# Weight rounding of a feed-forward layer moved within an attention stage, one VectorE operation per slot

## What is computed

```python
x = _layernorm(x + _L0_attn_ref(x, ...))   # 16 heads, causal, power-law decay
x = _layernorm(x + _L0_ffn_ref(x, w_gate, w_up, w_down))
x = _layernorm(x + _L1_attn_ref(x, ...))   # gated delta rule
x = _layernorm(x + _L1_ffn_ref(x, ...))

scores = jnp.einsum('bhnd,bhmd->bhnm', Q, K) / jnp.sqrt(jnp.float32(dk))
scores = scores + power_law_mask(N, DECAY_SCALE)[None, None]
attn = jax.nn.softmax(scores, axis=-1)

def fp4_quant_dequant(x):                  # blocks of 16 along the last dimension
    scale = jnp.max(jnp.abs(xb), axis=-1, keepdims=True) / 6.0
    scale = jnp.maximum(scale, jnp.float32(1e-12))
    xn = xb / scale
    idx = jnp.searchsorted(_MID, jnp.abs(xn))
    q = _GRID[idx] * jnp.sign(xn) * scale
```

## Time and profile before

| | |
|---|---|
| median of three runs | 3314.37 us (3314.29 to 3314.68) |
| profiled execution | 3316.07 us, span in the profile 3314.3 us |
| TensorE busy | 3003.8 us, 91% of the span |
| VectorE busy | 2307.2 us, 70% |
| ScalarE busy | 1222.2 us, 37% |
| GpSimd busy | 1022.4 us, 31% |
| mean granted TensorE clock | 0.96 of full |
| attention stage | about 0 to 658 us of the span |

### The profile page before, as it was taken

How to read it: one execution, slowest core, us unless ns; L and a number is a source line. 1 busy time by engine, 2 the same in 40 slices (tenths; PEclk the granted TensorE clock), 3 DMA queues, 4 the chain that set the end, 5 groups by cost and what they waited for, 6 DMA issues and landing times. The chain is left out here.

```text
span 3314.3 us, 81973 instructions
## 1 busy us (share of the span) xinstructions
PE 3003.8 (91%) x33019; PEld 2075.3 (63%) x33019; DVE 2307.2 (70%) x5231; ACT 1222.2 (37%) x2943; POOL 1022.4 (31%) x1495
## 2 busy tenths in 40 slices
PE   6999999599987999989999989999999999998897
PEld 3444444256655677677667767767776776776565
DVE  4666677778865776776776776777677677676466
ACT  2343333233333433343343343344344334332354
POOL 2454555348852221222221221221222122121011
PEclk8999999699988999999999999999999999998899
DMA  2111111000011110010010010000001001000000
GB/s 80 40 51 33 33 29 33 14 1 1 1 28 29 43 34 18 18 31 21 17 31 18 21 31 18 21 23 26 21 18 30 18 21 30 18 18 2 2 26 26
DMA packets 94040, 80.43 MB, mean 24 GB/s; under 512 B 54992, under 2 KB 68320, under 8 KB 93664
## 3 DMA queue, kind: packets, MB, share of 16 engines
q1 hardware_dynamic: 93664, 75.18, 8.4%
HBM read 57.70 MB, written 4.85 MB: 19 GB/s over the span
## 5 line engine op out<-in xcount | busy, mean ns | idle before, releaser
L1814 PE MATMUL gd_bk<-gd_xT,gd_wh 128*128 128x512 f32 x768 | 398.1, 628 | 22.1 <-DVE gd_L L1582 14.2
L480 DVE TENSOR_REDUCE at_nm<-at_ring 128x2 f32<-128x256 f32 (+3 forms) x256 | 199.2, 820 | 144.6 <-PE at_ring L623 144.6
L1528 DVE SCALAR_TENSOR_TENSOR gd_YK<-gd_bk,gd_cw,gd_YK 128x511 f32<-128x511 f32 (+2 forms) x384 | 282.8, 742 | 11.8 <-ACT gd_YK L1401 6.2
L1586 DVE COPY_PREDICATED gd_U<-gd_mU,gd_bk 128x256 f32<-128x256 int32 x320 | 140.9, 442 | 209.3 <-PE gd_bk L2016 149.5
L1994 PE MATMUL gd_bk<-gd_L,gd_NT 64*64 64x64 f32 x5120 | 212.5, 225 | 64.0 <-DVE gd_L L1588 41.3
L2011 PE MATMUL gd_bk<-gd_U,gd_ZS 64*64 64x64 f32 x5120 | 211.3, 225 | 39.4 <-ACT gd_ZS L1494 39.3
L1483 ACT COPY gd_O<-gd_bk 64x128 f32<-64x128 f32 x448 | 108.6, 260 | 356.9 <-PE gd_bk L1952 355.9
L1994 PEld LDWEIGHTS gd_bk<-gd_L,gd_NT 64*64 64x64 f32 x5120 | 177.9, 137 | 97.4 <-DVE gd_L L1588 55.8
L1494 ACT COPY gd_ZS<-gd_bk 128x256 f32<-128x256 f32 x320 | 115.2, 370 | 328.2 <-PE gd_bk L1994 324.9
L2011 PEld LDWEIGHTS gd_bk<-gd_U,gd_ZS 64*64 64x64 f32 x5120 | 178.4, 138 | 85.4 <-ACT gd_ZS L1494 43.5
L302 POOL TENSOR_TENSOR at_PT<-at_PT,at_dm 128x1024 f32<-128x1024 f32 (+3 forms) x128 | 198.0, 1547 | 10.7
(11 more groups left out here) (353 smaller groups left out, 6922.2 us busy)
## 6 DMA issues: line engine op xcount, KB each, us to landing
gd_wh<-in_L_attn_W_qkvz SPq DMA_DIRECT2D x64, 512.0 KB, 3.6
gd_gb<-gates SPq DMA_DIRECT2D x128, 64.0 KB, 3.3
X<-in_L_attn_x SPq DMA_DIRECT2D x8, 512.0 KB, 8.7
at_QT<-at_QS SPq DMA_DIRECT2D x128, 32.0 KB, 2.0
at_KT<-at_KS SPq DMA_DIRECT2D x128, 32.0 KB, 2.0
at_OC<-at_Ob SPq DMA_DIRECT2D x128, 32.0 KB, 2.0
at_RC<-inverse SPq DMA_DIRECT2D x128, 32.0 KB, 1.8
out_x<-X SPq DMA_DIRECT2D x8, 512.0 KB, 2.9
```

Of the source, the lines that this page charges most:

```text
L480: nc.vector.tensor_reduce(nm[v % 2][:, k, c0:c0 + HS + 1:HS], set_of(s, 2 + p)[:, :, 0:n], AX.X, ALU.max).then_inc(max_done, 1)
L1528: nc.vector.scalar_tensor_tensor(out[:, s:W], bank_[:, 0:W - s], cw[:, j, head(f, e), CONVK - 1 - s:CONVK - s], out[:, s:W], ALU.mult, ALU ...
L1586: last = nc.vector.copy_predicated(U[e][:, :, :], wide(mU[l]), chunks(A_[e], 1))
L1814: ins = nc.tensor.matmul(out[:, :], wh[e][:, k, col * DK:(col + 1) * DK], xT[:, k, :], start=k == 0, stop=k == DC - 1)
```

## The change

Three things, all in the attention:

- The steps start at unit 4 and not at unit 18, one in each slot, so that all 110 are done at unit 31, slot 1. Units 32 and 33 do none.
- Inside a slot the step stands between the decay addition (L452) and all else that VectorE does there; before, it stood after the row maxima, the query update and the y and V additions.
- The three loads of the raw weights are issued at units 0, 1 and 2 and not at 6, 8 and 10.

```diff
-    WUNIT = UNITS - 14
+    WUNIT = UNITS - 28
...
-                    if k == 0 and u in (6, 8, 10):
-                        ffn_load(sp, (u - 6) // 2)
+                    if k == 0 and u in (0, 1, 2):
+                        ffn_load(sp, u)
...
-                EARLY = (UNITS - WUNIT) * TPS
 
                 def weight_span(u, k):
 
-                    if u < WUNIT:
-                        return 0, 0
-                    if u < UNITS:
-                        i = (u - WUNIT) * TPS + k
-                        return i, i + 1
-                    if u == UNITS:
-                        a_ = EARLY + min(k, 3) * 8
-                        return (a_, a_ + 8) if k < 3 else (a_, a_)
-                    if u == UNITS + 1 and k < 3:
-                        a_, n_ = EARLY + 24, WALL - EARLY - 24
-                        return a_ + n_ * k // 3, a_ + n_ * (k + 1) // 3
-                    return 0, 0
+                    i = (u - WUNIT) * TPS + k
+                    return i, i + (0 <= i < WALL)
...
                         nc.vector.tensor_tensor(PT[s % RP][:, 0:2, 0:n], set_of(s, 1)[:, :, 0:n],
                                                 ld[:, 0:n].unsqueeze(1).broadcast_to([P, 2, n]), ALU.add).then_inc(add_done, 1)
+                    for i in range(*weight_span(u, k)):
+                        weight_step(i)
                     if k == 3 and has(u - 1) and u % 2 == 0:
...
-                    for i in range(*weight_span(u, k)):
-                        weight_step(i)
                     if g == 2 and seq(b - 1):
```

## The result

The changed kernel takes 3332.01 us (median of five runs, 3328.85 to 3336.46) against 3314.33 us before: slower by 0.55%, ratio 1.0055 with a 95% interval of 1.0041 to 1.007. The profiled execution took 3333.23 us around a span of 3331.5.

The account below looks back on a forecast made before the run. TensorE was taken to bound the attention, paced by first row maxima, a-scores, value product, max scores, next maxima. Costs of 17.2 and 11.5 less gains of 18.9 gave +9.8 us on 3314.37, so 3324.2; range 3305 to 3336.

Parts of the forecast that it names:

- the likeliest case: Four to seven clock drops with the waits as predicted: 3321 to 3330 us, chance 0.45.
- third rival: Each of eight stalls drops the clock and slow matmuls push slot 1's addition into L302: +20.5, 3335 us, chance 0.15.
- Cost 1: Steps ahead of the maxima wait for GpSimd's running operation in units 4 to 28: 17.2 us, bounds 6 and 21.
- Cost 2: Stalls in eight units make TensorE's clock drop, 2.3 us a drop: 11.5 us, bounds 0 and 18.4.
- forms 0 to 3: Of ten repeating step kinds, a reduce and three small operations on 32 columns; a small one in unit 12 costs nothing.
- five of eight: Of eight units with stalls of 1.3 to 2 us, five were taken to drop the clock: 11.5 us.
- The rival without drops: Waits as predicted but no clock drops: -1.7 us, 3312.7 us, chance 0.25.
- Gain 1: The tail without the 54 steps of units 32 and 33: 9.2 us, from waits of 4.9 and 3.7 plus 0.6.
- Gain 2: Units 18 to 27: what the steps in their old places cost comes back, 7.7 us.
- Gain 3: Units 28 to 31: a short step hides better there than the old one, 2 us by estimate, bounds 0 and 4.
- The first rival: No clock drops, waits as predicted: -1.7 us, 3312.7 us; with up to three drops still within 7 us; chance 0.25.
- hidden steps: The wait goes to GpSimd and costs under 6 us, without drops: 3301.5 us, or 3295.5 with no cost; chance 0.15.

Follow-up runs that it names:

- scalar-operation kernel: The changed kernel with 109 of its 110 steps replaced by a scalar multiply and maximum on 32 columns, weights not rounded: 3326.83 us, ratio 1.0043.
- the kernel with both GpSimd operations short: The changed kernel with GpSimd's product L302 and its residual addition L309 both cut to one column: 3297.02 us, ratio 0.9954.
- the planned one: The changed kernel without steps in three slots, two in slots with long idle time, steps in units 2 to 27, loads one unit earlier: 3295.08 us, ratio 0.9943.

## Why the prediction was right, and where it was off

The time, 3332.0, is in the range and on the side that I forecast, and the mechanism is the one that I gave. The size is not: +17.7 us came where my sum said +9.8, and 3332 lies outside the likeliest case's own 3321 to 3330, near the third rival (3335). Two terms were too small, Cost 1 and the number of clock drops in Cost 2. By its steps:

- **What bounds.** First maxima -> a-scores -> next maxima is the order that sets the pace: shown by unit 8, and by the three slots whose step, moved behind the maxima, costs nothing.
- **The wait for GpSimd.** Shown from both sides. Other VectorE operations in the same place cost 0.7 us (reciprocal) and 6.7 us (reduce) between unit 4 and unit 28 in place of 34, and the same steps beside short GpSimd operations cost 7.1. The part that the steps cost by their own length is up to 7 us, most of it by single clock drops.
- **The term that was mis-sized is Cost 1, its list of forms.** I took forms 0 to 3 as free. The scalar operations of forms 1 and 3 wait as well; only reduce and reciprocal do not. The trace of before held no meeting of one with a long product, and I put all small ones with the reduce. It did hold a sign that I passed over, three meetings with the short L299. The longest, in unit 31, took twice the usual 0.17 us and ended just as that L299 (612.84 + 0.41 = 613.25) did:

```profile
612.93 0.35 DVE L399 TENSOR_SCALAR prep<-prep 128x32 f32<-128x32 f32 x1
```

  Against clean units, in us:

| unit | forms in slots 0, 1 | predicted, with drop | measured |
|---|---|---|---|
| 4, 24 | 0, 1 | 0.3 each | 0.88 each |
| 6, 26 | 8, 9 | 4.3 each | 2.66, 3.49 |
| 8 | 6, 7 | 4.5 | 4.16 |
| 10 | 4, 5 | 3.7 | 3.57 |
| 12 | 2, 3 | 0 | 3.10 |
| 14 | 0, 1 | 0.15 | 2.04 |
| 16 | 8, 9 | 4.8 | 4.42 |
| 18 | 6, 7 | 4.1 | 4.09 |
| 20 | 4, 5 | 4.2 | 4.18 |
| 22 | 2, 3 | 0 | 1.05 |

  Units 4, 12, 14, 22 and 24 make 8 us with 0.75 predicted. Units 8, 10, 16, 18 and 20 agree within 0.4; units 6 and 26 came 1.6 and 0.8 lower, with shorter falls of the clock.
- **Cost 2, the clock.** The price of a drop was 2.3 in the sum and 2.24 by units 10 and 14 of the scalar-operation kernel. The count was too low: I took five of eight, and each of the eight fell, the units 12 and 14 too (in units 6, 14 and 26 the fall lasted half as long as in unit 8). The step that failed is the reading of the earlier trace rows behind the five of eight, "1.24 us idle at 594.40 left the clock at 1.00": that window ends at 596, and TensorE had its next stall right behind it:

```profile
599.59 1.33 PE L561 MATMUL at_ring<-at_QT,at_KT 32*128 32x256 f32 x8 [3.81 <-DVE at_PT L452]
```

  The granted clock was 0.61 from 598 to 602 and 0.50 from 600 to 604. So this row showed no stall that the clock outlived; the two that could be read, 0.98 and 2.03 us, were both followed by a drop. In unit 8, too, the clock was still 1.00 up to 208 and fell at 209, some 2 us behind the stall.
  The rival without drops is refuted for this kernel: 1.14 us of stall in unit 8 was followed by half clock. The Trainium skill, "TensorE: Matmul & The Clock Gate", section "Why this matters for your kernels", names only longer idle gaps than these as what lowers the clock in the middle of a kernel. The traces here do not agree: half clock followed with no gap above 1.14 us in unit 8, and with none above 0.52 us in unit 6 of the kernel with both GpSimd operations short. That a stall need not bring a drop is shown as well, by unit 10 of the scalar-operation kernel and, in the changed kernel itself, by unit 22: its stall of 1.11 us left the clock up, one of 0.91 in unit 12 did not. The length of the stall alone does not decide; what does was not found.
- **Gain 1** was 9.2, measured 11.2 in the profile: the two waits as predicted (5.1 for 4.9 and 3.6 for 3.7, and 0.8 for the added 0.6), the rest the second output product at the higher clock, 1.8, which the sum did not have. By itself the tail is worth 8 to 9 us.
- **Gain 2**, 7.7: came back, since units 19, 21, 23, 25 and 27 are clean and the others' loss is counted from clean.
- **Gain 3**, with unit 28's cost, was to be +2.5 us; +3.3 came.
- **The first rival and the second** (hidden steps) did not come. Of the third one half came, each of the eight stalls dropped the clock; the other half, stalls that push slot 1 into L302, did not: the slot 1 steps of units 8, 16, 20 and 28 took 0.90, 0.89, 0.50 and 0.68 us, they met the short L299 at most.

With forms 1 and 3 counted (+7) and all drops (+7) my sum would have been some 3338 without the larger gain in the tail, 3336 with it. The measured 3332 is below, mostly by units 6 and 26, where half clock lasted half as long as in unit 8. That these shorter falls and the tail took back part of the two errors is luck.

## What to carry to other kernels

Where an engine idles is not enough to place filler work: ask whose result the next wait takes, and what GpSimd does at that moment if the filler is an operation of VectorE that waits for it. A filler in front of the operation that feeds the bound engine must fit, with its own wait, into the idle time; behind that operation it only needs the slack of the next one. Count the fillers by the kind of operation first and by length second: 109 operations of 0.17 us cost 32 us more over a kernel than 109 of 0.34 us, and reduces of up to 0.68 us cost some 7 us between unit 4 and unit 28. And when a row is to show that a stall did no harm to the clock, read the windows behind it too.

## What the runs showed of the hardware

- A scalar multiply and maximum on 128 x 32 waits for GpSimd's running product and so took up to 1.71 us; a reciprocal on the same columns (0.338 to 0.348 us in 109) and a reduce on 512 columns (at most 0.678 in 110) do not.
- The same stall of 1.12 us, in the same place of the loop, left TensorE's clock up in unit 10 and was followed by half clock in unit 14; the second cost 2.24 us more, for a fall of some 7 us.
- Half clock also followed where TensorE had idled no longer than 0.52 us at a time (unit 6 of the kernel with both GpSimd operations short, 170.5 to 177.5), while a stall of 1.11 us in unit 22 of the changed kernel left it up.
- Within one kernel the five runs spread over 7.6 us (3328.85 to 3336.46) in the changed kernel and over 2.3 us in the planned one, which has hardly a stall in the steady part. That the clock's drops make this spread was not tried.
